# Layer 1 of a two-layer recurrent network, worked off by pairs of sequences instead of one sequence at a time

## The reference

```
xn = _layernorm(x)
s = recurrence(xn)                  # layer 0: a long convolution
g = silu(moe32(xn) + shared(xn))    # layer 0: 32 experts, 4 for each token
x = x + s * g
xn = _layernorm(x)
q, k, v = xn @ wq.T + bq, xn @ wk.T + bk, xn @ wv.T + bv
s = softmax(q @ k.T * scale) @ v    # layer 1: attention inside a sequence
hmid = gelu(einsum('th,eih->tei', xn, w_fc), approximate=False)
y = einsum('tei,ehi->teh', hmid, w_proj)
g = silu(einsum('teh,te->th', y, gates))  # 8 experts, 2 gates a token that aren't 0
x = x + s * g
```

## Time and profile before

| What | us |
|---|---|
| median of 3 runs (lowest to highest) | 483.96 (482.9 to 487.52) |
| the profiled execution, its own time | 484.2 |
| its span | 482.5 |
| layer 1, from its first matmul (313.37) to the end of the span | 169.1 |
| each pair of layer 1, from one `q`, `k` product to the next but one | 22.1, 20.4, 20.6, 19.6, 21.7, 20.0, 18.7, 18.5 |
| from the end of the last attention output's products (475.0) to the end | 7.5 |

### The profile page before, as it was taken

How to read it: one execution, slowest core, us unless ns; L and a number is a source line. 1 busy time by engine, 2 the same in 40 slices (tenths; PEclk the granted TensorE clock), 3 DMA queues, 4 the chain that set the end, 5 groups by cost and what they waited for, 6 DMA issues and landing times.

```text
span 482.5 us, 8882 instructions
## 1 busy us (share of the span) xinstructions
PE 385.3 (80%) x2576; PEld 342.4 (71%) x2576; DVE 330.0 (68%) x1150; ACT 260.7 (54%) x497; POOL 288.6 (60%) x333
## 2 busy tenths in 40 slices
PE   0666898852299999995999989769888898898895
PEld 0664787641189889884899989758777686777774
DVE  6989787869346566550147877847897989884633
ACT  2250134300156666652666766567658776668673
POOL 6995777777777777763777777157777770000000
PEclk9996998976589999997999999989999999999999
DMA  6899991111436656545466666322322220100010
GB/s 175 265 356 298 326 398 65 52 51 47 132 122 201 203 194 190 196 148 173 138 208 220 204 190 202 111 65 56 84 82 77 75 74 29 43 24 22 23 34 22
DMA packets 48205, 67.26 MB, mean 139 GB/s; under 512 B 8841, under 2 KB 25634, under 8 KB 48162
## 3 DMA queue, kind: packets, MB, share of 16 engines
q1 hardware_dynamic: 39970, 49.93, 31.8%
q0 software_dynamic: 8192, 16.79, 12.0%
HBM read 28.93 MB, written 35.65 MB: 134 GB/s over the span
## 4 chain that ended last, share of the span: by engine, by line
PE 34%; DVE 26%; POOL 14%; issue 11%; ACT 9%; DMA 5%; SPq 1%; DVEq 0%; ACTq 0%; POOLq 0%
POOL slot_rows L560 14%; PE ps L749 11%; PE ps L740 5%; DMA rows<-slot_rows 4%; PE ps L724 4%; DVE trig L1333 3%; PE ps L732 3%; ACT L1106 2%; PE ps L862 2%; ACT sg L978 2%; DVE mx L1467 2%; DVE rows L1484 1%; PE ps L895 1%; PE ps L591 1%; DVE act L1317 1%
## 5 line engine op out<-in xcount | busy, mean ns | idle before, releaser
L560 POOL DMA_INDIRECT slot_rows<-xn_tok,slot_of x128 | 135.1, 1055 | 42.9 <-issue 38.7
L574 POOL DMA_INDIRECT onehot<-expert_rows,slot_of x64 | 61.3, 957 | 40.7 <-DMA expert_rows<-zeros 21.8
L1317 DVE TENSOR_TENSOR act<-sg,ps 128x384 f32<-128x384 f32 x48 | 26.6, 554 | 81.1 <-ACT sg L978 80.6
L574 POOL DMA_INDIRECT route_tmp<-expert_rows,slot_of x64 | 62.1, 970 | 19.5 <-issue 19.5
L740 PE MATMUL ps<-w_dn,actT 96*128 x384 | 51.0, 275 | 1.5 <-ACT actT L996 1.5
L740 PEld LDWEIGHTS ps<-w_dn,actT 96*128 96x128 f32 x384 | 46.8, 192 | 2.1 <-issue 2.0
L978 ACT ACTIVATE sg<-ps 128x384 f32<-128x384 f32 x48 | 23.5, 490 | 38.3 <-PE ps L749 38.3
L724 PE MATMUL ps<-ident,rows 128*128 128x128 f32 x192 | 31.9, 292 | 12.3 <-DMA rows<-slot_rows 10.6
L749 PE MATMUL ps<-w_gu,raw_fc 128*128 x192 | 37.5, 341 | 0.0
L724 PEld LDWEIGHTS ps<-ident,rows 128*128 128x128 f32 x192 | 23.8, 149 | 18.5 <-DMA rows<-slot_rows 13.8
L987 ACT COPY zeros<-ps 128x512 f32<-128x512 f32 x48 | 28.1, 586 | 15.6 <-PE ps L740 15.6
(11 more groups left out here) (224 smaller groups left out, 894.7 us busy)
## 6 DMA issues: line engine op xcount, KB each, us to landing
slot_rows<-zeros SPq DMA_DIRECT2D x12, 1024.0 KB, 12.0
rows<-slot_rows SPq DMA_DIRECT2D x48, 256.0 KB, 3.3
expert_rows<-zeros SPq DMA_DIRECT2D x48, 256.0 KB, 2.1
x_tok<-in_L_attn_x_dram SPq DMA_DIRECT2D x8, 256.0 KB, 5.8
slot_rows<-xn_tok,slot_of POOLq DMA_INDIRECT x128
hs_t<-xn_tok SPq DMA_DIRECT2D x16, 128.0 KB, 2.1
out_dram<-raw_fc SPq DMA_DIRECT2D x16, 128.0 KB, 1.8
w_dn<-in_L_ffn_w_down_dram SPq DMA_DIRECT2D x1, 1536.0 KB, 15.1
```

The source lines that it names most:

```text
L560: g.indirect_dma_start(out=slot_rows[r], out_offset=bass.IndirectOffsetOnAxis(ap=slot_of[:, n:n + 1], axis=0), in_=xn_tok[:, r * HT + t, : ...
L574: g.indirect_dma_start(out=gath[b % 4][:, j, :], out_offset=None, in_=expert_rows[r], in_offset=bass.IndirectOffsetOnAxis(ap=slot_of[:, n: ...
L1317: v.tensor_tensor(act[u][:].rearrange("p (a b) i -> p a b i", a=2), sg[u][:].rearrange("p (a b) i -> p a b i", a=2), ps[:, 1 + 2 * u:3 + 2 ...
```

## The change

The loop of layer 1 runs over eight pairs `p` on every engine. A pair has a bank for the attention of each sequence (`ATT`), in which `q` and `k`, scores, transposed probabilities and attention output follow one another, and two banks for the hidden units of each (`HID`); the expert sums of a pair (`SUM`) lie in two of these four. ScalarE takes both exponentials and then both gelus, `finish` and the tanh of the sum run once for a pair over twice the elements, one DMA stores a pair, and `load_xn` and the second copy of the normalized rows (`xn1T_pair`) are gone. The weighted sum of the gathered rows is four large operations for a pair (`weigh_rows`, `sum_rows`) instead of 16 short ones, in layer 0 too, and the gather buffers hold two pairs instead of four sequences. `NORM_AT`, `summed` and `gated` give way to `TURN_AT`, `GATES_AT` and calls written out in VectorE's loop; `link_beside` is no longer used. In the cut diff below lines that start with + are new; most removed lines are left out, since the functions of the kernel before stand above.

```diff
-NORM_AT = {-1: 3, 3: 4, 5: 5, 8: 6, 10: 7}
+TURN_AT = {0: 3, 3: 4, 4: 5, 5: 6, 6: 7}
+GATES_AT = {0: 1, 3: 2, 4: 3, 5: 4, 6: 5}
...
+        ATT, HID, SUM, VAL, ROW = (4, 5), (0, 2), (1, 2), 6, 7
+        expert_sum = ps[:, SUM[0]:SUM[1] + 1, 0:SEQ]
...
-            for b in range(NSEQ):
-                r = b // (NSEQ // NH)
-                if b % (NSEQ // NH) == 0:
+            for p in range(FSEQ):
+                r = p // (FSEQ // NH)
+                if p % (FSEQ // NH) == 0:
-                if b >= 4:
-                    pool.wait_ge(c_f, b - 3)
-                for j in range(2 * TOP0):
-                    n = b * 2 * TOP0 + j
-                    g.indirect_dma_start(
-                        out=gath[b % 4][:, j, :], out_offset=None, in_=expert_rows[r],
-                        in_offset=bass.IndirectOffsetOnAxis(ap=slot_of[:, n:n + 1], axis=0)).then_inc(g_in[b % 4], 16)
+                if p >= 2:
+                    pool.wait_ge(c_f, p - 1)
+                for j in range(GT):
+                    for k in range(TOP0):
+                        n = (p * GT + j) * TOP0 + k
+                        g.indirect_dma_start(
+                            out=gath[p % 2][:, j, k, :], out_offset=None, in_=expert_rows[r],
...
+            def rows_of(p, u):
+                return xn_tok[:, 4 * p + 2 * u:4 * p + 2 * u + 2, :]
+            def expert_sums(p):
+                for u in range(2):
+                    pe.wait_ge(d_hs, 2 * p + u + 1)
+                    for j in range(2):
+                        for c in range(CH1):
+                            mm = pe.matmul(ps[:, SUM[u], j * P:(j + 1) * P], hg[u][:, c, j * P:(j + 1) * P],
+                                           prT[:, c, :], start=(c == 0), stop=(c == CH1 - 1))
...
+            for p in range(FSEQ):
+                turning = TURN_AT.get(p)
+                pe.wait_ge(c_xn_kept, p + 1)
+                if p:
+                    pe.wait_ge(d_os, p)
+                for u in range(2):
+                    for j in range(2):
+                        mm = pe.matmul(ps[:, ATT[u], j * SEQ:(j + 1) * SEQ], w1T[:, j, :], rows_of(p, u),
+                                       start=True, stop=True)
+                    mm.then_inc(d_qk, 1)
+                if p:
+                    pe.wait_ge(d_vs, p)
+                for t in range(4):
+                    mm = pe.matmul(ps[:, VAL, t * P:(t + 1) * P], xn_tok[:, 4 * p + t, :], w1T[:, 2, :],
+                for u in range(2):
+                    pe.wait_ge(d_qks, 2 * p + u + 1)
+                        mm = pe.matmul(ps[:, ATT[u], j * SEQ:(j + 1) * SEQ], qk_sb[u][:, 0, j * P:(j + 1) * P],
+                                       qk_sb[u][:, 1, :], start=True, stop=True)
+                    mm.then_inc(d_s, 1)
+                if p:
+                    expert_sums(p - 1)
+                turn_gates(p)
+                if turning is not None:
+                    pe.wait_ge(d_gTs, p + 1)
+                    turn_xn(turning)
+                for u in range(2):
+                    pe.wait_ge(d_p, 2 * p + u + 1)
+                        for j in range(2):
+                            mm = pe.transpose(ps[:, ATT[u], k * SEQ + j * P:k * SEQ + (j + 1) * P],
+                                              pr[u][:, j, k * P:(k + 1) * P], ident[:])
+                    mm.then_inc(d_pT, 1)
+                if turning is not None:
+                    gate_logits(turning).then_inc(c_lg, 1)
+                if p:
+                    pe.wait_ge(d_mg, p)
+                for u in range(2):
+                    for c in range(CH1):
+                        mm = pe.matmul(ps[:, HID[u] + c // 2, (c % 2) * SEQ:(c % 2 + 1) * SEQ], fcT[:, c, :],
+                                       rows_of(p, u), start=True, stop=True)
+                    mm.then_inc(d_h, 1)
+                pe.wait_ge(d_vs, p + 1)
+                for u in range(2):
+                    pe.wait_ge(d_pTs, 2 * p + u + 1)
+                    for j in range(2):
+                        for k in range(2):
+                            mm = pe.matmul(ps[:, ATT[u], j * P:(j + 1) * P], pT[u][:, k, j * P:(j + 1) * P],
+                                           v_sb[:, 2 * u + k, :], start=(k == 0), stop=(k == 1))
+                pe.wait_ge(d_gTs, p + 1)
+                for u in range(2):
+                    pe.wait_ge(d_hg, 2 * p + u + 1)
+                    for c in range(CH1):
+                        mm = pe.matmul(ps[:, HID[u] + c // 2, (c % 2) * SEQ:(c % 2 + 1) * SEQ], expert_sel[:, c, :],
+                                       gT[p % 2][:, 0:2 * SEQ][:, u * SEQ:(u + 1) * SEQ], start=True, stop=True)
+                    mm.then_inc(d_gb, 1)
+                if turning is not None:
+                    pe.wait_ge(c_lgs, turning + 1)
+            expert_sums(FSEQ - 1)
...
+                a.activation(mth[:], expert_sum, ACT.Tanh, scale=0.5).then_inc(d_mth, 1)
+            for p in range(FSEQ):
+                turning = TURN_AT.get(p)
+                for u in range(2):
+                    sc.wait_ge(d_qk, 2 * p + u + 1)
+                    if p:
+                        sc.wait_ge(d_s, 2 * p + u - 1)
+                    for j in range(2):
+                        last = a.activation(qk_sb[u][:, j, :], ps[:, ATT[u], j * SEQ:(j + 1) * SEQ], ACT.Identity,
+                                            bias=bqk[:, j:j + 1])
+                    last.then_inc(d_qks, 1)
+                sc.wait_ge(d_v, p + 1)
+                if p:
+                    sc.wait_ge(d_o, p)
+                a.copy(v_sb, bank(VAL).rearrange("p (a d) -> p a d", d=P)).then_inc(d_vs, 1)
+                for u in range(2):
+                    sc.wait_ge(d_nmx, 2 * p + u + 1)
+                    for j in range(2):
+                        last = a.activation(pr[u][:, j, :], ps[:, ATT[u], j * SEQ:(j + 1) * SEQ], ACT.Exp,
+                                            bias=nmx[:, 2 * u + j:2 * u + j + 1], scale=SCALE,
+                                            accum_out=den[:, 2 * u + j:2 * u + j + 1])
+                    last.then_inc(d_p, 1)
+                if p:
+                    tanh_moe(p - 1)
+                sc.wait_ge(d_gT, p + 1)
+                a.copy(gT[p % 2][:, 0:2 * SEQ], ps[0:3 * E1, ROW, :]).then_inc(d_gTs, 1)
+                if turning is not None:
+                    copy_xn(turning)
+                for u in range(2):
+                    sc.wait_ge(d_pT, 2 * p + u + 1)
+                    a.copy(pT[u][:].rearrange("p a b -> p (a b)") if u == 0 else pT[u].rearrange("p a b -> p (a b)"),
+                           bank(ATT[u])).then_inc(d_pTs, 1)
+                if turning is not None:
+                    logits_between(turning, turning + 1)
+                for u in range(2):
+                    sc.wait_ge(d_h, 2 * p + u + 1)
+                    a.activation(hg[u], ps[:, HID[u]:HID[u] + 2, :].rearrange("p a (b n) -> p (a b) n", b=2),
+                                 ACT.Gelu).then_inc(d_hg, 1)
+                if p in GATES_AT:
+                    tanh_gates(GATES_AT[p])
+                if p in (1, 2, 4, 5):
+                    tanh_f({1: 4, 2: 5, 4: 6, 5: 7}[p])
+            tanh_moe(FSEQ - 1)
...
+            def weigh_rows(p):
+                dve.wait_ge(g_in[p % 2], 16 * GT * TOP0 * (p // 2 + 1))
+                w = top_w[:, p * GT * TOP0:(p + 1) * GT * TOP0].rearrange("p (t k a) -> p t k a", t=GT, a=1)
+                link(v.tensor_tensor(gath[p % 2], gath[p % 2], w.to_broadcast([P, GT, TOP0, P]), ALU.mult))
+            def sum_rows(p):
+                g = gath[p % 2]
+                link(v.tensor_tensor(g[:, :, 0:2, :], g[:, :, 0:2, :], g[:, :, 2:4, :], ALU.add))
+                link(v.tensor_tensor(f_sb, g[:, :, 0, :], sh_tok[:, p * GT:(p + 1) * GT, :], ALU.add))
+                v.tensor_tensor(f_sb, f_sb, g[:, :, 1, :], ALU.add).then_inc(c_f, 1)
...
+            make_gates(0)
+            def gate_hidden(p):
+                for u in range(2):
+                    dve.wait_ge(d_gb, 2 * p + u + 1)
+                    v.tensor_tensor(hg[u], hg[u], ps[:, HID[u]:HID[u] + 2, :].rearrange("p a (b n) -> p (a b) n", b=2),
+                                    ALU.mult).then_inc(d_hs, 1)
+            def maxima(p):
+                for u in range(2):
+                    dve.wait_ge(d_s, 2 * p + u + 1)
+                    m = slice(2 * u, 2 * u + 2)
+                    link(v.tensor_reduce(mx[:, m], bank(ATT[u]).rearrange("p (a n) -> p a n", a=2), AX.X, ALU.max))
+                    v.tensor_scalar(nmx[:, m], mx[:, m], -SCALE, None, ALU.mult).then_inc(d_nmx, 1)
+            def finish(p):
+                u = p % 2
+                dve.wait_ge(d_mth, p + 1)
+                v.scalar_tensor_tensor(out=mg[:], in0=mth[:], scalar=1.0, in1=expert_sum,
+                                       op0=ALU.add, op1=ALU.mult).then_inc(d_mg, 1)
+                dve.wait_ge(d_mg, p + 1)
+                dve.wait_ge(d_os, p + 1)
```

(58 more changed lines are left out.)

299 lines of the change are left out of this document (50 added, 249 removed).

## The result

The changed kernel takes 508.43 us as a median of four runs (505.66 to 512.58) where the kernel before takes 485.74 beside it (482.9 to 489.34): ratio 1.0453, 95% interval 1.0393 to 1.0513. The profiled execution took 507.26 us, its span is 505.5, 23.0 over the span before. The forecast was +14.25: right in sign, 8.75 short, above its range.

What follows compares the result with a forecast made beforehand. Pairs bound by VectorE's lumps of preparation, plain pairs near TensorE's own work. Pairs 4.05, end 2.9, layer 0 2.8 and clock 4.5 give +14.25 on 484.2: 498.4 us, range 489.2 to 505.

Steps and rivals of the forecast that it cites:

- The formula of a pair: Layer 1: a pair takes max(9.45, X + 6.5) + max(5.65 or 7.8, 1.65 + A) + 1.2 us.
- X: VectorE work behind `weigh_output`, ahead of the next pair's `gate_hidden` and maxima; 2.95 us free, all above paid in full.
- Place decides, not VectorE's share: Layer 1: the question is where VectorE's preparation lies; pairs sum to 165.65 us against 161.6.
- place A: VectorE work between `finish` and `weigh_output`; free if under 4.0 us, or 6.15 where TensorE also turns a later pair.
- The end: After the last `weigh_output`: gated units, expert sums, tanh, `finish` and store take 10.4 us against 7.5, +2.9.
- The clock in pairs 5 and 6: Layer 1: TensorE idles 5.9 and 7.6 us, then runs expert sums at half rate: 2 x 2.25 = 4.5 us, bounds 0 and 6.75.
- Pair 0: Layer 1's first pair: 18.0 us against 22.1 now, first products at half clock, bounds 16.5 to 19.5.
- Layer 0: `weigh_rows` waits for all 16 gathers of a pair: 1.6 us in pair 2, +2.8 in all, bounds 0 and 3.5.
- Pair 3: In layer 0: last gather lands at 306.1, `hidden` at 308.35 instead of 305.52; +2.8 in all, first shift included.
- 4.05: Layer 1's eight pairs: sum of 165.65 us against 161.6 now, before the end and the clock.
- The rival of 505 us: Much slower: clock also falls behind pair 2 and around pairs 3 and 4, 3 x 2.25 us more; chance 0.12.
- The table loads: Layer 1, ScalarE: 16 of 32 go, 1.28 us each, 20.5 us; worth set by TensorE's chain, not their sum.

Runs made afterwards that it cites:

- the spread version: Changed kernel without gathers of pairs 4 to 7, VectorE's layer 1 preparation in three places, two tanh ahead of gelus: 494.48 us, 1.0186; with gathers, stalling: 726.48 us, 0.9868.
- halves: Changed kernel with layer 0's sums of a pair in two halves, each waiting for 8 gathers: 501.89 us, ratio 1.0372; on a stalling chip 739.25 us, 1.0078.

## Why the prediction came out short

- **The formula of a pair: right.** Seven of eight pairs are within 0.3 us of it, the clock included. `weigh_rows` took 2.29 (priced 2.25), the sum over 1,024 elements 1.22, X in pair 6 12.3 (12.35). The large operations gain nothing by being large: 5.0 us for the sums of a pair, where the short ones and their copies took 4.8.
- **Place decides, not VectorE's share: right**, and now shown: 6.9 us more in place A cost nothing, and the same work spread took 11.7 us from pairs 1 to 6.
- **The end: right.** From the last pair's end at 495.0 to 505.5, 10.5 (10.4).
- **The clock in pairs 5 and 6: right.** Priced 4.5; taking it away gave 4.2 on the stalling chip and 4.2 on the other. The clock also fell behind pair 2, from 379.0 to 385.8, where only the rival has it. There it was nearly free, since TensorE was waiting for VectorE: pairs 2 and 3 took 22.2 and 21.1 for 21.95 and 21.05.
- **"Pair 0 ... its first products run at half clock as they do now; 16.5 to 19.5 bounds it": failed.** It was 21.1. I counted the half clock that layer 0 leaves behind, and not a second one behind TensorE's wait for ScalarE's copy of the first gates. That is the first half of the rival "the clock also falls", at a place that it did not name. Cost 3.1 us: in the spread version, with the first half clock and without the second, the pair took 18.0, as priced. The Trainium skill ("TensorE: Matmul & The Clock Gate", HAM oscillation — how this bites in real kernels) warns of longer idle gaps of TensorE than this one; here 2.30 us was followed by half clock in this kernel and not in the spread version, so the trace decides, and it doesn't give a rule.
- **Layer 0, "the gathers land at 287.2; the operation ends at 289.4": failed.** I carried the landing over from the kernel before. It came at 289.3, 2.1 us later, and the wait was followed by half clock, which I had priced only in layer 1. The transposes that were to come 1.6 us later (`L732` at 288.34 before, `L699` at 292.26 now) came 3.9 later, and at 300.4, where the half clock ends, TensorE was 7.7 behind: 2.3 us are the late landing and 3.8 the half clock. Pair 3, priced at 1.2 more, added 0.3. Together the shift was 8.0 us for 2.8. That the wait for all 16 is the cause is shown from both sides: the wait added to the kernel before makes its layer 0 3.9 us longer, halves in the changed one make it about 6 us shorter. That GpSimd issued late because of the large operations is argued from the rows below.
- **The sum:** 2.8 + 5.2, 4.05 + 3.1, 2.9, 4.5 are 22.55 of 23.0. The rival of 505 us came nearest in the number, but for other places of the clock. Its bounds of layer 0 (0 to 3.5) excluded what happened.
- **The table loads:** with them the new order would take 529 us. So they gave 21 us, and the rest of the change took 44. The prediction reads the load as starting 1.04 us after the exponentials; that is from the start of the first (470.14), and the last of them ends at 471.16, 0.02 before the load.

## What to carry to other kernels

Before merging short steps into large ones, ask what the merged step must wait for and what stands behind it on its engine: here half of the data was there, and a wait for all of it held up TensorE. Count a lump by its place: between an engine's result and the work that it waits for anyway it was free, ahead of the operation that feeds TensorE it was paid in full beyond the first 2.95 us, although VectorE was busy for only 63% of that pair. And where a change gives TensorE a new wait on the chain, price the half clock behind it as a bound in every stage, not only behind the longest waits.

## What the hardware showed that I had not expected

A gather that GpSimd issued while VectorE ran the multiplication of 2,048 elements took two to over three times its usual 0.94 us: 1.89, 2.04 and 2.63 at 289.79 (above) in layer 0, and in pair 3 of layer 1, on GpSimd and then on VectorE:

```profile
377.03 3.13 POOL L541 DMA_INDIRECT onehot<-expert_rows,slot_of  x1 [0.30 <-issue]
```

```profile
377.06 2.28 DVE L1296 TENSOR_TENSOR route_tmp<-route_tmp,top_w 128x2048 f32<-128x2048 f32 x1
```

In all six slow cases of this trace it ended 0.81 or 0.82 us after the multiplication did, wherever in it it had begun: here 380.16 after 379.34, above 292.42 after 291.61. One that began at 250.57, 0.03 us behind the start of a multiplication, kept its 0.94. From the first gather to the last of pair 2 GpSimd never waits for data in layer 0, so each such delay moves all that follow: the issue times over 0.94 add up to 3.2 us by 286.05 in the changed kernel and to 0.7 before, which with the 0.7 us that it started later make the 3.2 us by which the last gather of pair 2 came late (282.84 to 286.05). The Trainium skill ("Advanced Engine Details and Errata", VectorE Performance Modes) says that VectorE's second SBUF port is shared with GpSimd and names instructions in two-port modes; here the slow issues lie beside an operation with two inputs in SBUF. No run separated this from other causes.

TensorE's granted clock fell to 0.50 after short waits: 2.04 us in the kernel before with the added wait, 2.30 us in pair 0, in two traces. After the same 2.30 us it did not fall in the spread version, so I can give no rule.

The stalls of 20 to 40 us were a state of the chip at a time and not of the kernel: a chip that showed them in the first four kernels had none in four others some 40 minutes later, where the kernel before took 485 us again. They covered waits of 5 us completely, so that four runs on a wait for data said nothing by their times, until the trace of the same stretch was read.
